# Linear attention: the order of VectorE's residual, values and inner norm

## The reference

```python
q = x @ Wq + bq
k = (x @ Wk + bk) @ Wc @ We          # 4 heads, each repeated 4 times
v = (x @ Wv + bv) @ Wc @ We
qf, kf = elu(q) + 1, elu(k) + 1
kv_cum = jnp.cumsum(jnp.einsum('bhsf,bhsd->bhsfd', kf, v), axis=2)
num = jnp.einsum('bhsf,bhsfd->bhsd', qf, kv_cum)
den = jnp.einsum('bhsf,bhsf->bhs', qf, jnp.cumsum(kf, axis=2))[..., None] + EPS
o = (num / den).transpose(0, 2, 1, 3).reshape(b, s, D) @ Wo + bo
y = residual + o
mu, var = jnp.mean(y, -1, keepdims=True), jnp.var(y, -1, keepdims=True)
return (y - mu) / jnp.sqrt(var + LN_EPS) * gamma + beta
```

## Time and profile before

| what | value |
|---|---|
| median of 3 runs | 7300.41 us |
| profiled execution, its own time | 7294.51 us |
| its span | 7292.4 us |
| the stage's first mask to its last (32 masks) | 926.5 to 1186.9 us |
| in 926 to 1187: PE, DVE, ACT, POOL busy | 222.77, 213.30, 107.17, 189.15 us |
| mean granted TensorE clock there | 0.84 of full speed |

### The profile page before, as it was taken

How to read it: one execution, slowest core, us unless ns; L and a number is a source line. 1 busy time by engine, 2 the same in 40 slices (tenths; PEclk the granted TensorE clock), 3 DMA queues, 4 the chain that set the end, 5 groups by cost and what they waited for, 6 DMA issues and landing times. The chain is left out here.

```text
span 7292.4 us, 189527 instructions
## 1 busy us (share of the span) xinstructions
PE 6507.4 (89%) x74836; PEld 3973.7 (54%) x74836; DVE 5360.5 (74%) x8933; ACT 4055.2 (56%) x6024; POOL 2820.5 (39%) x1680
## 2 busy tenths in 40 slices
PE   7989987887697989989999779989899999989998
PEld 5767665444442333333333356666576767667676
DVE  7877576665556999999999856677577777768544
ACT  3556343665446777777777745455344444456433
POOL 3321175332214888888888601165021212211000
PEclk9999978999888999999999989999999999999999
DMA  1000000000001222222222100000000000000000
GB/s 29 0 21 13 3 11 8 3 3 2 14 2 52 76 73 75 75 80 77 76 75 76 51 12 13 9 31 3 12 2 2 2 2 2 2 15 14 2 0 23
DMA packets 115881, 190.04 MB, mean 26 GB/s; under 512 B 38661, under 2 KB 74746, under 8 KB 114970
## 3 DMA queue, kind: packets, MB, share of 16 engines
q1 hardware_dynamic: 112218, 183.47, 7.9%
q10 hardware_dynamic: 3264, 0.54, 0.1%
HBM read 173.87 MB, written 7.98 MB: 25 GB/s over the span
## 5 line engine op out<-in xcount | busy, mean ns | idle before, releaser
L2600 POOL TENSOR_TENSOR m_dBx<-m_dtx,m_Bs 128x1024 f32<-128x1024 f32 x515 | 1165.8, 2283 | 227.3 <-DVE m_hs L2965 185.2
L2965 DVE TENSOR_TENSOR_SCAN m_hs<-m_ps_dA,m_dBx 128x512 f32<-128x512 f32 x1030 | 1200.5, 1207 | 56.4 <-POOL m_dBx L2600 55.8
L2719 PE MATMUL m_ps_y<-m_yc,ident 128*128 128x512 f32 x2060 | 1021.6, 619 | 0.0
L2824 ACT ACTIVATE m_ps_dA<-m_dt,m_A 128x504 f32<-128x504 f32 x1030 | 682.0, 678 | 427.1 <-DVE m_hs L2965 424.4
L2096 POOL TENSOR_TENSOR a_s<-a_s,a_den 128x1024 f32<-128x1024 f32 x128 | 243.5, 1902 | 1123.9 <-DVE a_den L2142 1123.9
L2976 DVE TENSOR_TENSOR m_yc<-m_hs,m_ps_C 128x1024 f32<-128x1024 f32 x515 | 616.3, 1197 | 1.3 <-PE m_ps_C L2700 1.3
L2719 PEld LDWEIGHTS m_ps_y<-m_yc,ident 128*128 128x128 f32 x2060 | 350.5, 190 | 357.0 <-issue 357.0
L2700 PE MATMUL m_ps_C<-m_parts,m_sel 48*128 48x512 bf16 x516 | 199.8, 387 | 175.7 <-DVE m_yc L2976 175.6
L2700 PEld LDWEIGHTS m_ps_C<-m_parts,m_sel 48*128 48x128 bf16 x516 | 47.7, 92 | 566.9 <-DVE m_yc L2976 421.2
L625 POOL TENSOR_TENSOR c_kbd<-c_kf,c_hmask 128x1024 f32<-128x1024 f32 x66 | 125.0, 1893 | 515.9 <-ACT c_kf L534 492.0
L2140 DVE TENSOR_REDUCE a_den<-a_s 128x16 f32<-128x1024 f32 x128 | 156.0, 1219 | 207.0 <-ACT a_s L2047 207.0
(11 more groups left out here) (748 smaller groups left out, 16025.2 us busy)
## 6 DMA issues: line engine op xcount, KB each, us to landing
m_Bs<-BC_rows SPq DMA_DIRECT2D x258, 512.0 KB, 3.5
c_kvb<-in_ctxT SPq DMA_DIRECT2D x68, 128.0 KB, 2.1
c_kvb<-in_ctxT SPq DMA_DIRECT2D x17, 256.0 KB, 2.7
out_dram<-X SPq DMA_DIRECT2D x1, 4096.0 KB
BC_rows<-m_low SPq DMA_DIRECT2D x33, 64.0 KB, 2.7
part_rows<-m_split SPq DMA_DIRECT2D x33, 48.0 KB, 1.7
m_parts<-part_rows SPq DMA_DIRECT2D x33, 48.0 KB, 1.7
m_piece<-BC_rows SPq DMA_DIRECT2D x33, 32.0 KB, 1.7
```

The source lines that it names most:

```text
L2600: return nc.gpsimd.tensor_tensor(to, one, other, ALU.mult)
L2719: last = nc.tensor.matmul(ps_y[:, m, :], C.ident[:], of[:, m, :], start=s == 0, stop=s == NS - 1)
L2824: nc.scalar.activation(seqs(ps_dA[:, h % 3, :]), seqs(dt[:, par, m, :]), ACT.Exp, scale=A[:, second, m, s:s + 1]).then_inc(decay, 1)
L2965: nc.vector.tensor_tensor_scan(hs[:, s % HS, m, :], ps_dA[:, (2 * s + m) % 3, :], dBx[:, s % BX, m, :], 0.0, ALU.mult, ALU.add).then_inc(s ...
```

## The change

In a slot of DVE, residual(w-2) comes directly after normalise(w-1), and diagonal_values(w) directly after it, without the drain between. One drain follows, and then one batch, joint(w-2), which works on three units: it centres unit w-3 (two instructions, L1207 of the new file), takes the statistics of y of unit w-2 (two) and of the new x of unit w-4 (two), drains, aggregates both (four), adds unit w-3 to x (two, L1226), drains, and writes unit w-4's results to C.MV with a maximum of mv2 with itself (128x4, L1230) in every slot. Before, a copy of 128x8 did that in every other slot. The new x of a unit is summed up one slot later than before. The other engines' programs are the same.

```diff
--- before.py
+++ after.py
@@ -891,7 +891,7 @@
         gamma, beta = sb("gamma", [P, D]), sb("beta", [P, D])
         st, mv = sb("st", [P, UT, 6]), sb("mv", [P, TPG, 2])
         eps, rs2 = sb("eps", [P, 1]), sb("rs2", [P, 2, UT])
-        st2, mv2 = sb("st2", [P, UT, 6]), sb("mv2", [P, TPG, 2])
+        st2, mv2 = sb("st2", [P, UT, 6]), sb("mv2", [P, UT, 2])
 
         ps_s, ps_a, ps_b = ps("ps_s", [P, RG, 512]), ps("ps_a", [P, 2, UC]), ps("ps_b", [P, 512])
         ps_c, ps_t = ps("ps_c", [P, 512]), ps("ps_t", [P, 512])
@@ -1195,77 +1195,71 @@
                 dve.wait_ge(out_done, w + 1)
                 rows_ = C.Y[:, bass.ds(w * UT, UT), :]
                 tt(rows_, tiles(t_on), rows_, ALU.add).then_inc(out_read, 1)
-                dve.drain()
 
             def row(t, n):
                 return t[:, bass.ds(n, 1), :].rearrange("p a d -> p (a d)")
 
-            def row_sums(w, u):
-                for t in range(UT):
-                    nc.vector.bn_stats(st[:, t, :], row(C.Y, w * UT + t))
-                dve.drain()
-                for t in range(UT):
-                    last = nc.vector.bn_aggr(mv[:, u * UT + t, :], st[:, t, :])
-                last.then_inc(var_ready, 1)
-
-            def add_rows(w, u):
-
-                dve.wait_ge(rs_ready, w + 1)
-                for t in range(UT):
-                    y = row(C.Y, w * UT + t)
-                    nc.vector.scalar_tensor_tensor(y, y, mv[:, u * UT + t, 0:1], gamma[:], ALU.subtract, ALU.mult)
-                dve.drain()
-                for t in range(UT):
-                    x = row(C.X, w * UT + t)
-                    nc.vector.scalar_tensor_tensor(x, row(C.Y, w * UT + t), rs2[:, u, t:t + 1], x, ALU.mult, ALU.add)
-
-            def new_sums(w, i, u):
-
-                for t in range(UT):
-                    nc.vector.bn_stats(st2[:, t, :], row(C.X, w * UT + t))
-                dve.drain()
-                for t in range(UT):
-                    nc.vector.bn_aggr(mv2[:, u * UT + t, :], st2[:, t, :])
-                if u == UPG - 1:
+            def joint(w, par, centre=True, sums=True, new=True):
+
+                if centre:
+                    for t in range(UT):
+                        y = row(C.Y, (w - 1) * UT + t)
+                        nc.vector.scalar_tensor_tensor(y, y, mv[:, (1 - par) * UT + t, 0:1], gamma[:], ALU.subtract, ALU.mult)
+                if sums:
+                    for t in range(UT):
+                        nc.vector.bn_stats(st[:, t, :], row(C.Y, w * UT + t))
+                if new:
+                    for t in range(UT):
+                        nc.vector.bn_stats(st2[:, t, :], row(C.X, (w - 2) * UT + t))
+                dve.drain()
+                if sums:
+                    for t in range(UT):
+                        last = nc.vector.bn_aggr(mv[:, par * UT + t, :], st[:, t, :])
+                    last.then_inc(var_ready, 1)
+                if new:
+                    for t in range(UT):
+                        nc.vector.bn_aggr(mv2[:, t, :], st2[:, t, :])
+                if centre:
+                    dve.wait_ge(rs_ready, w)
+                    for t in range(UT):
+                        x = row(C.X, (w - 1) * UT + t)
+                        nc.vector.scalar_tensor_tensor(x, row(C.Y, (w - 1) * UT + t), rs2[:, 1 - par, t:t + 1], x, ALU.mult, ALU.add)
+                if new:
                     dve.drain()
-                    nc.vector.tensor_copy(C.MV[:, bass.ds(i * TPG, TPG), :], mv2[:])
-
-            def slot(w, i, u, weigh=True, project=True, finish=True):
+                    new_rows = C.MV[:, bass.ds((w - 2) * UT, UT), :]
+                    tt(new_rows, mv2[:], mv2[:], ALU.max)
+
+            def slot(w, u, weigh=True, project=True, finish=2):
                 mask(w, u)
                 if weigh:
                     normalise(w - 1)
-                if finish:
-                    add_rows(w - 3, 1 - u)
                 if project:
                     residual(w - 2)
                 diagonal_values(w, u)
                 if project:
-                    row_sums(w - 2, u)
-                if finish:
-                    new_sums(w - 3, i - 1 - (1 - u), 1 - u)
-
-            slot(0, 0, 0, False, False, False)
-            slot(1, 0, 1, True, False, False)
-            slot(2, 1, 0, True, True, False)
-            slot(3, 1, 1)
+                    dve.drain()
+                    joint(w - 2, u, finish > 0, True, finish > 1)
+
+            slot(0, 0, False, False, 0)
+            slot(1, 1, True, False, 0)
+            slot(2, 0, True, True, 0)
+            slot(3, 1, True, True, 1)
             with dve.Fori(2, C.NG) as i:
                 for u in range(UPG):
-                    slot(i * UPG + u, i, u)
+                    slot(i * UPG + u, u)
             n = last_unit
             residual(n - 1)
             normalise(n)
-            row_sums(n - 1, 0)
-            add_rows(n - 2, 1)
             dve.drain()
-            new_sums(n - 2, C.NG - 2, 1)
+            joint(n - 1, 0)
             residual(n)
-            row_sums(n, 1)
-            add_rows(n - 1, 0)
             dve.drain()
-            new_sums(n - 1, C.NG - 1, 0)
-            add_rows(n, 1)
+            joint(n, 1)
             dve.drain()
-            new_sums(n, C.NG - 1, 1)
+            joint(n + 1, 0, True, False, True)
+            dve.drain()
+            joint(n + 2, 1, False, False, True)
+
 
 
 class Front:
```

## The result

After takes 7334.07 us (median of 6 runs, 7327.32 to 7346.45), before 7301.26 in the same series (6 runs, 7296.68 to 7310.95): ratio 1.0046, 95% interval 1.0034 to 1.0057, so 33 us slower. Forecast were 7315 and a range of 7284 to 7337. Most of the loss, though, lies where the forecast put zero, far behind the changed block.

What follows compares the result with a forecast made beforehand. It took DVE's own work (7.74 us per full-clock slot) to bound the stage; 28 slots at +0.52 us gave +14.6 on 7294.5, so 7309, plus 5.9 for a median: 7315 us, range 7284 to 7337.

Steps and rivals of the forecast that it cites:

- Code before the fourth mask and after the last hardly changes; I take it as zero: Outside the stage's 28 slots between fourth and last mask, the change was given no effect on time: zero.
- DVE's own offsets: Times after a slot's mask without POOL: residual 3.24, bias's end 4.45, next mask 7.35 us; mean slot 7.48 instead of 7.74.
- POOL's offset: POOL's next round (from L1126) starts 6.37 us after the bias's end, so L1126 comes 1 to 3 us after the mask.
- The kind of meeting: POOL holds up the moved centring and additions: pairs of 1.2 us and more for 0.61, full-clock slots 8.7 to 9.5.
- The write: In the slot's end, the write to C.MV meets POOL's instructions and takes up to 0.7 us instead of 0.17.
- one sentence on the rows: A DVE instruction that starts inside a POOL TENSOR_TENSOR ends 0.15 us after it.
- The net of +14.6 for the stage: Slots between fourth and last mask take 9.05 us against 8.53: 28 x 0.52 = +14.6 us.
- PE's waits: DVE's 12 waits for PE's weighted values at low clock, 14.5 us, are gone in the longer slots.
- Rival 1, the free way: In the slots, moved instructions slip past POOL: gain 18 us (7 plus 11 of PE's waits), 7282 us; chance 0.23.
- rival 2: Longer slots leave PE at 1.2 GHz more often; slots become 9.9 us, +39 us, 7339 us; chance 0.13.
- Rival 3: Hardly fewer pauses between DVE's instructions in a slot: forecast rises by 3 us, inside the range; given no chance.
- by the row and not by the rule: DVE over L1126 loses little (pair 0.73 us), by profile; full blocking by the skill's rule would put 8 us on top.

Runs made afterwards that it cites:

- e1: The changed kernel with 3 drains added at the end of the linear attention's VectorE program (3866 instructions, as before): 7306.91 us, ratio to before 1.0004.
- e2: The kernel before with 125 drains added at the end of the linear attention's VectorE program (3991 instructions): 7338.64 us, ratio to before 1.0052.
- e9: The changed kernel with 2 drains added at the end of the linear attention's VectorE program (3865 instructions): 7339.94 us, ratio to before 1.0051.
- e4: The changed kernel, padded to 3866 VectorE instructions, with POOL's L1128 and L1130 only writing constants, reading nothing from SBUF: 7270.87 us, ratio to before 0.9956.
- e5: New DVE slot order: previous slot's C.MV write and centring ahead of the bias, additions right behind it, statistics and aggregates last: 7261.31 us, ratio to before 0.995.
- e7: The changed kernel without the write to C.MV and its drain, padded by 17 drains to 3866 VectorE instructions: 7265.49 us, ratio to before 0.9953.
- e6: The changed kernel with centring and additions put back directly behind normalise, joint statistics and each slot's write kept: 7298.47 us, ratio to before 1.0.
- e3: The kernel before with only residual and values' bias moved ahead of add_rows (3865 VectorE instructions): 7359.82 us, ratio to before 1.0075.
- e8: The kernel before with POOL's sum and product (L1128, L1130) replaced by constant writes that read nothing from SBUF: 7310.22 us, ratio to before 1.001.

## Why the prediction was right in direction, and for the wrong reason

- The failed step is "Code before the fourth mask and after the last hardly changes; I take it as zero". It is right of the instructions, and wrong of their place: worth, by the differences of the ratios times 7301, 31 us (after against e1), 38 (e2 against before, its 125 drains included), 34 (e9 against e1).
- That 7334 lies inside the range, on the forecast side, is luck. With the code where it was, the change is worth 0.0004 (−0.0006 to 0.0014), that is −4 to +10 us, and the range would have held that too.
- DVE's own offsets held: residual 3.23 after the mask (forecast 3.24), the bias's end 4.41 (4.45). With nothing held, the slot is 7.42 in e4 (7.48).
- POOL's offset held in one slot of four: its next round begins 6.38 after the bias's end (6.37; from 1082.83 to 1089.21) there, and about 7.0, 8.3 and 10.5 after it in the other three. So L1126 comes 1.6, 5.8, 5.4 and 3.4 us after the mask in turn, where 1 to 3 was named.
- The kind of meeting held: additions of 2.22 where 1.2 and more were named, the two slots at full clock 8.41 and 9.22 (8.7 to 9.5, 9.05 in the middle). The write was mis-sized: up to 1.60, where 0.7 was named. And one sentence on the rows was too wide: the copy and the write end 0.02 to 0.03 us after POOL's instruction (969.18 for 969.15 in the earlier trace rows), only instructions of the centring and the additions 0.15 after it.
- The net of +14.6 for the stage was mis-sized: it measured +1.9 in the trace. I took every slot for one at full clock. But the clock still falls, POOL's round is late behind such a stretch, and one slot in four then comes free at 7.32, which makes the mean 8.59 over the 28. PE's waits went nearly as forecast (1.6 us left of 14.5).
- Rival 1, the free way, was not what happened, but its price was too small: in e4, e5 and e7, with nothing or (e7) 7 us held, the low clock goes as well, and the gain is 32 us (e4), 34 (e7) and 37 (e5) by the ratios, not 18.
- Of rival 2 the lower clock came (0.81 for 0.85), its long slots only as single ones (9.93 once). Rival 3 fell: by it the free slot would be 7.60, and e4 has 7.42.
- For L1126 I had gone by the row and not by the rule. The additions of e5 in its later part take 0.61. A centring that lies over its start is held, but only for its first 0.8 us (0.97 for the pair at 1014.16 in after; 0.78 for one at 968.54 in e7), so the Trainium skill's rule (SBUF — State Buffer, Who interferes with whom) that the loser is blocked to the end does not fit L1126, while it fits L1128, L1130, L1118 and L1119.

## What to carry to other kernels

Before calling code behind an edit unchanged, ask whether a large loop of the same engine follows, and after a run compare the instruction packets and the idle "issue" before a loop's first instruction: an edit's own effect is only read with the code position restored. Where two engines share SBUF, write down the partner's round with its pauses, and put the instructions with two SBUF inputs into these, those with one tensor read elsewhere. The clock can change with the length of a slot, so judge an order by its run, not by the sum of its pieces.

## What the runs showed of the hardware

- Seven branches back, each followed by a stop of 3.9 to 4.5 us, come or go with one instruction ahead of the loop (3865 stops, 3866 not). The Trainium skill, Runtime: NRT & Kernel Launch, Instruction fetch mechanics, says that a taken branch to code outside the pages an engine holds makes it wait for a fetch. The trace agrees: five packets come with each stop. By 0.79 less 0.51 MB in 35 packets a packet is 8 KB on this queue, where the Trainium skill's page has blocks of 16 KiB; e2, where 125 instructions more act as 3 fewer do, fits the 8 KB.
- Why this loop and not the one before it was not tried. An estimate from counting the kernels' instructions: ahead of this loop of 302 instructions stand 2259 of VectorE's in before, 2263 in e6 and 2303 in e5, which have no stops, and 2258 (e3, e9), 2256 (after) and 2384 (e2), which have them. If a packet holds 128 and one begins behind number 2259, the loop lies in three packets without the stops and in four with them, and the first loop (304, beginning 490 earlier) in three in every kernel. The place of that border was chosen to fit, so this is not shown.
- A copy is held by POOL's plain write (0.92 for 0.17 in e8), an instruction with two SBUF inputs is not (0.58 for a pair in e4).
- The kernels with slots of 7.5 us and less (e4, e5, e7) kept the clock at 0.99 or 1.00 through 960 to 1150, those at 8.4 and more had 0.81 to 0.87. Which of the two makes the other was not settled.
- Centring and additions that take one input from PSUM, which might avoid the meetings, were not tried: all of PSUM is in use.
